# Three PSUM banks for the scan and three for the rest, the convolution in mid-unit, and u by one Silu pass, in a Mamba block with a quantised branch

## The chip, the cores and the metric

One core of one Trainium2 chip. The time is device microseconds of one launch, the median of 3 runs. Engines: TensorE (PE in the profile, PEld its weight loads), VectorE (DVE), ScalarE (ACT), GpSimd (POOL), and SyncE (SP), which here only issues DMAs. Each engine runs its own program in order; semaphores tie them together.

## The reference, cut to what matters

Eight sequences of 512 tokens and 128 channels, all in float32. Each is normalised over its channels (xn). xn then goes through a Mamba layer in both directions and through a Hadamard transform, a 4-bit rounding of each token and a ternary weight. The outputs are added to x.

```python
def _mamba_dir(xz, ...):                     # d_inner 256, state 16, dt_rank 8
    u = silu(causal_conv(x, 4 taps) + bias)
    x_dbl = einsum('bdl,kd->bkl', u, xproj_w)            # 8 rows for dt, 16 for B, 16 for C
    delta = softplus(dtproj_w @ x_dbl[:, :8] + dt_bias)
    dA = exp(einsum('bdl,dn->bdln', delta, A))
    dBx = einsum('bdl,bnl,bdl->bdln', delta, Bm, u)
    h = scan(dA, dBx)                                    # h[t] = dA[t] * h[t-1] + dBx[t]
    y = einsum('bdln,bnl->bdl', h, Cm) + Dp * u
    return y * silu(z)
xq = quantize(xn @ H)            # round(x / s), clipped to -8..7, times s; s = max|x| / 7 of a token
out = x + (out_f + out_b) @ out_proj_w.T + xq @ ternary(weight).T
```

## The kernel before, in words

**Units, slots, tiles.** The work goes in 16 units, U = 2b + d: sequence b, direction d (even units forward, odd ones backward). A unit has 8 slots s (128 channels by 4 of the 16 states), a slot has 4 tiles j of 128 partitions x 512 tokens (32 channels x 4 states), so a unit has 32 tiles. In this text k = 4s + j counts the tiles of a unit. V is the unit after U, W the one after V.

**A tile's way.** TensorE puts delta·B·u of a tile into a bank of the PSUM tensor b_ps. In slots 0 and 1 it copies delta·u there (`copies`, L864) and VectorE multiplies by B (`times_b`, L557, two tiles at once). In slots 2 to 7 it transposes four blocks (L879) of dbx_t, made in token-major form from the transposed delta·u (du_t): three state rows of four by ScalarE (`inputs_t`, L405, three instructions for each of four blocks c), the fourth by GpSimd (L688). ScalarE computes the decay exp(delta·A) (`decays`, L416) into da, a pair of buffers of 4 tiles, so it can be 8 tiles ahead. VectorE scans (L569) into hst, a ring of 4 slots. GpSimd multiplies two tiles at a time by C (`states_times_c`, L678). TensorE sums over the states into y (`sum_states`, L894).

**The next unit's preparation** runs in between. TensorE convolves (`conv`, L792, four taps for each half h of the channels) into pb, a PSUM tensor of two banks; ScalarE makes a sigmoid from a Tanh and a Copy (`u_sigmoid`, L330, L332); VectorE makes u from both (`make_u`, L539). TensorE projects it (`x_proj`, L799; `steps`, L811). The softplus goes over Abs and Relu (L351, L352), Exp (L377), a Copy (L379) and Ln (L383) on ScalarE; then VectorE has three passes over 1024 columns (`log1p`, L543 and L545; `delta`, L549). GpSimd makes delta·u (`make_du`, L694), TensorE transposes it (`du_transposed`, L819), ScalarE copies the result to du_t (`keep_dut`, L388). delta goes to HBM and comes back replicated four times (`spread` on SyncE, L234), which rep needs before V's first decay.

**Once for each sequence**, odd units have the rounding: `hadamard` (L833, TensorE), `token_max` (L514, VectorE), the scale on GpSimd (L727), `quantize` (L516, VectorE, nine instructions in a row), `project` (L848) and the residual (L580). Even units have the normalisation of the next sequence and the gate silu(z) (`z_proj`, `z_sigmoid`, `gates`), in both cases with the two banks of pb.

**What sets the order** is code written out by hand: each engine has a function `unit` with `if s == ...` lines that say after which slot half a step stands. Sequences 1 to 6 run in a hardware loop (`batches`); the first and last are written out. Everything that goes through pb waits until what was in the bank is read; in b_ps each of the 4 banks belongs to one j.

Of the kernel before, what the change touches and what calls it, by code (L numbers as in the profile page):

```python
# [35 lines left out]
def build(nc, x, win_t, wz_t, conv_w, cols, xproj_t, dt_t, a_log, wout_t, ffn_w, had, ident_d, sum_sel_d, spread_d, out):
    ctx = ExitStack()
    with ctx:
# [40 lines left out]
        xq = xn  # L79
# [37 lines left out]
        x_loaded = sem("x_loaded")  # L117
        xres_loaded = sem("xres_loaded")
# [63 lines left out]
        def batches(eng, body):
            body(0)
            with eng.Fori(1, NB - 1) as i:
                body(i)
            body(NB - 1)

        def first(b):
            return isinstance(b, int) and b == 0

        def last(b):
            return isinstance(b, int) and b == NB - 1
# [3 lines left out]
        def _(sp):  # L196
            def rows(ap, b):
                return ap[bass.ds(b, 1)].rearrange("b (c p) d -> p (b c) d", p=P)

# [846 lines left out]
```

## Time and profile before

| | us |
|---|---|
| Median of 3 runs (972.45 to 978.01) | 977.39 |
| The profiled execution, its own time | 976.08 |
| Its span | 974.0 |
| Mean granted TensorE clock, as a share of full speed | 0.864 |

The span runs from the first to the last instruction of the profiled execution; 2.1 us of its time lie outside. In the views below, "us" ahead of a row is the time since the span's start, [x <-y] is the time that the engine sat idle before the row and what ended it, "xN" the number of instructions merged. A float32 matmul of 512 columns shows as two records. Successive instructions of an engine overlap by about 0.1 us, so the distance between starts is the price in a row of them, and the duration a little more.

### The profile page before, as it was taken

The numbers are of one execution on the slowest core, as the hardware profiler recorded it, in microseconds if no ns is written. First come the engines' busy times: TensorE is split into PE (matmuls) and PEld (weight loads), VectorE is DVE, ScalarE is ACT, GpSimd is POOL, SyncE is SP. The second block draws the span as 40 slices with busy tenths as digits, with TensorE's granted clock in tenths as the row PEclk, the third lists the DMA queues.
The fourth block names the chain that finished last, engine by engine and source line by source line (L and its number), as shares of the span: only waits on it lengthen the run. The fifth ranks groups of instructions, "written<-read, shape, count | busy, mean of one in ns | idle before, by whom it ended". The sixth has DMA issues, their size and how long they took to land.

```text
span 974.0 us, 13835 instructions
## 1 busy us (share of the span) xinstructions
PE 765.9 (79%) x3873; PEld 384.4 (39%) x3873; DVE 800.2 (82%) x838; ACT 782.1 (80%) x1454; POOL 750.2 (77%) x454
## 2 busy tenths in 40 slices
PE   3486977689786977979689697878978697797994
PEld 1233443343433435334353344434443343433452
DVE  2278988898788878888888887889878887897995
ACT  2599995899878987789967998589986898878970
POOL 2159887788768977789787887878886798777994
PEclk9788988889787988979889797988978798897797
DMA  3424225070620607024070512507052070702400
GB/s 91 113 66 118 48 79 107 4 163 4 141 55 30 135 3 172 24 70 91 30 166 3 126 38 70 124 3 162 3 126 68 10 154 3 172 14 68 95 7 27
DMA packets 51433, 72.53 MB, mean 74 GB/s; under 512 B 6704, under 2 KB 19920, under 8 KB 51408
## 3 DMA queue, kind: packets, MB, share of 16 engines
q1 hardware_dynamic: 50976, 71.97, 31.6%
q10 hardware_dynamic: 432, 0.26, 0.1%
q8 instruction: 12, 0.20, 0.1%
q14 instruction: 13, 0.11, 0.0%
HBM read 60.68 MB, written 11.53 MB: 74 GB/s over the span
## 4 chain that ended last, share of the span: by engine, by line
POOL 29%; issue 27%; PE 18%; ACT 15%; DVE 8%; DMA 2%; POOLq 1%; SPq 0%; DVEq 0%; ACTq 0%
POOL hst L678 22%; PE pb L792 5%; DVE hst L569 5%; ACT da L416 4%; POOL dbx_t L688 4%; PE b_ps L879 4%; ACT dbx_t L405 2%; PE y L894 2%; PE b_ps L864 1%; PE y L891 1%; POOL t_log L694 1%; ACT xn L308 1%; PE pb L856 1%; DVE b_ps L557 1%; PE pb L811 1%
## 5 line engine op out<-in xcount | busy, mean ns | idle before, releaser
L678 POOL TENSOR_TENSOR hst<-hst,c_rep 128x1024 f32<-128x1024 f32 x256 | 600.6, 2365 | 170.8 <-DVE hst L569 170.1
L569 DVE TENSOR_TENSOR_SCAN hst<-da,b_ps 128x512 f32<-128x512 f32 x512 | 586.3, 1202 | 43.1 <-ACT da L416 21.4
L879 PE MATMUL b_ps<-ident,dbx_t 128*128 128x128 f32 x1536 | 246.6, 301 | 158.3 <-DVE hst L569 157.4
L416 ACT ACTIVATE da<-rep,neg_a 128x511 f32<-128x511 f32 x512 | 336.2, 710 | 5.8 <-DVE hst L569 3.8
L879 PEld LDWEIGHTS b_ps<-ident,dbx_t 128*128 128x128 f32 x1536 | 181.0, 151 | 281.2 <-DVE hst L569 255.7
L405 ACT ACTIVATE dbx_t<-du_t,b_t 128x256 f32<-128x256 f32 x576 | 247.0, 496 | 2.5 <-PE b_ps L879 1.7
L894 PE MATMUL y<-hst,sum_sel 128*32 128x512 f32 x1024 | 148.9, 657 | 3.0 <-POOL hst L678 3.0
L792 PE MATMUL pb<-xnt,conv_wt 128*128 128x512 f32 x256 | 121.0, 617 | 0.8 <-ACT xnt L316 0.8
L688 POOL TENSOR_TENSOR dbx_t<-du_t,b_t 128x1024 f32<-128x1024 f32 x48 | 91.3, 1903 | 2.7 <-ACT du_t L388 2.7
L864 PE MATMUL b_ps<-t_log,spread_sel 32*128 32x512 f32 x256 | 73.4, 679 | 14.3 <-POOL t_log L740 9.8
L557 DVE TENSOR_TENSOR b_ps<-b_ps,b_rep 128x1024 f32<-128x1024 f32 x64 | 78.0, 1219 | 5.4 <-PE b_ps L864 5.4
L792 PEld LDWEIGHTS pb<-xnt,conv_wt 128*128 128x128 f32 x256 | 47.2, 194 | 71.6 <-issue 71.4
L388 ACT ACTIVATE du_t<-pb 128x512 f32<-128x512 f32 x32 | 18.8, 589 | 59.7 <-PE pb L819 59.7
L891 PE MATMUL y<-u,skip 128*128 128x512 f32 x64 | 54.8, 1008 | 0.0
L539 DVE SCALAR_TENSOR_TENSOR u<-pb,col,t_exp 128x512 f32<-128x512 f32 x32 | 23.9, 746 | 36.9 <-ACT t_exp L332 36.9
L894 PEld LDWEIGHTS y<-hst,sum_sel 128*32 128x32 f32 x1024 | 21.3, 114 | 76.6 <-issue 51.6
L543 DVE SCALAR_TENSOR_TENSOR pb<-pb,t_log 128x1024 f32<-128x1024 f32 x15 | 18.5, 1233 | 39.8 <-ACT t_log L383 39.8
L864 PEld LDWEIGHTS b_ps<-t_log,spread_sel 32*128 32x128 f32 x256 | 21.7, 194 | 68.4 <-DVE hst L569 40.7
L351 ACT ACTIVATE t_exp<-pb,col 128x512 f32<-128x512 f32 x30 | 20.6, 688 | 34.2 <-PE pb L811 34.2
L330 ACT ACTIVATE t_exp<-pb,half_bias 128x512 f32<-128x512 f32 x32 | 21.9, 684 | 31.3 <-PE pb L792 31.3
L694 POOL TENSOR_TENSOR t_log<-t_pos,u 128x1024 f32<-128x1024 f32 x15 | 35.5, 2369 | 0.0
L799 PE MATMUL pb<-u,xproj 128*128 128x512 f32 x64 | 33.1, 641 | 2.3 <-DVE u L539 2.2
(111 smaller groups left out, 588.5 us busy)
## 6 DMA issues: line engine op xcount, KB each, us to landing
rep<-d_scr SPq DMA_DIRECT2D x128, 256.0 KB, 9.1
c_rep<-bc_scr SPq DMA_DIRECT2D x64, 256.0 KB, 4.8
d_scr<-t_pos SPq DMA_DIRECT2D x15, 512.0 KB, 3.0
b_rep<-bc_scr SPq DMA_DIRECT2D x64, 64.0 KB, 2.2
x_ln<-x SPq DMA_DIRECT2D x8, 256.0 KB, 3.3
x_res<-x SPq DMA_DIRECT2D x8, 256.0 KB, 2.8
out<-x_res SPq DMA_DIRECT2D x8, 256.0 KB, 7.1
conv_wt<-conv_w SPq DMA_DIRECT2D x2, 512.0 KB, 5.8
```

Source lines behind the costliest of these rows:

```text
L405: ins = nc.scalar.activation(dbx_t[(NX * d + q - 1) % 2][:, c, :, r, :], du_t[d][:, c, :, :], ACT.Copy, scale=b_t[d][:, c, n:n + 1])
L416: nc.scalar.activation(da[s % 2][:, j, 1:L], rep[d][h][:, j, 1:L], ACT.Exp, scale=neg_a[:, d, h, j, q:q + 1]).then_inc(decay_done, 1)
L557: nc.vector.tensor_tensor(b_ps[:, two, :], b_ps[:, two, :], b_rep[d][:, :].unsqueeze(1).broadcast_to([P, 2, L]), ALU.mult).then_inc(b_scal ...
L569: nc.vector.tensor_tensor_scan(hst[s % RING][:, j, :], da[s % 2][:, j, :], b_ps[:, j, :], 0.0, ALU.mult, ALU.add).then_inc(scan_done, 1)
L678: nc.gpsimd.tensor_tensor(hst[s % RING][:, two, :], hst[s % RING][:, two, :], c_rep[d][:, q:q + 1, :].broadcast_to([P, 2, L]), ALU.mult).t ...
L688: nc.gpsimd.tensor_tensor(dbx_t[(NX * d + q - 1) % 2][:, :, :, POOL_R, :], du_t[d][:, :, :, :], by_c, ALU.mult).then_inc(bm_pool, 1)
L694: nc.gpsimd.tensor_tensor(du[:, :, :], t_pos[:, :, :], u[d][:, :, :], ALU.mult).then_inc(du_ready, 1)
L792: ins = mm(pb[:, 1 - h, :], conv_wt[d][:, k, P * h:P * (h + 1)], window, start=k == 0, stop=k == TAPS - 1)
L864: mm(b_ps[:, j, :], spread_sel[at, :], du[at, h, :], start=True, stop=True).then_inc(t_filled, 1)
L879: ins = tr(b_ps[:, j, P * c:P * (c + 1)], dbx_t[(NX * d + q - 1) % 2][:, c, NJ * h + j, :, :].rearrange("p r e -> p (r e)"), ident[:, :])
L891: mm(y[:, n, :], skip[:, d, n, :], u[d][:, n, step], start=False, stop=False, skip_group_check=True)
L894: ins = mm(y[CB * j:CB * (j + 1), h, :], sum_sel[:, :], hst[s % RING][:, j, step], start=d == 0 and q == 0, stop=d == 1 and q == NQ - 1, s ...
```

## The change

- **Banks.** b_ps has 3 banks (BANKS) instead of 4, taken in turn by the running number of the tile, so TensorE may fill tile k + 3 once tile k is scanned. pb has 3 banks instead of 2. `times_b` does one tile (512 columns) at a time, one tile ahead of the scan.
- **Grain.** All engines' `unit` functions now count tiles k from 0 to 31, and place at most a few steps between two tiles. No hardware loop: the 16 units are written out.
- **Convolution.** For unit W, two units ahead, tap by tap at TensorE's k = 9, 10, 12, 13 (half 0, bank 2) and 14, 16, 17, 18 (half 1, bank 0). Before, whole halves stood at the end of U (slot 7).
- **u.** One Silu on ScalarE for each half, both at k = 23, with no VectorE pass; the Tanh, the Copy and `make_u` on VectorE are gone. The column half_bias goes too.
- **delta·u's transposes.** At TensorE's k = 20 and 22 (even U) or 20 and 21 (odd U); `keep_dut` at ScalarE's k = 25 and 27. Half n uses bank 1 + n.
- **Softplus.** Abs and Relu at k = 8 and 9, Exp at 10, the Copy at 11, Ln at 12; on VectorE the three passes at k = 9, 10 and 11 (before: in slot 3). `make_du` on GpSimd one slot half after.
- **Inputs of slots 6 and 7** (q = 3) at ScalarE's k = 17 to 20, those of V's slots 2 and 3 at 26, 27, 29 and 31.
- **Rounding.** xq now lies in x_ln. token_max, scale, inverse, round, clip and scale stand alone after VectorE's k = 24 to 29, `hadamard` at TensorE's k = 22, into bank 2. The scale is computed on VectorE.
- **Normalisation** is a sequence earlier; x of sequence 1 is loaded into x_res. Its `statistics` stand at VectorE's k = 20 of even units, its Ln and Exp (k = 12) and `normalize` (k = 22) in odd ones. `load_x` on SyncE stands behind `spread`.
- **Loads.** On SyncE the B and C loads stand ahead of the wait for delta. `x_proj` has 64 output rows instead of 128.

The core of the diff:

```diff
+G = NJ * SLOTS
+UNITS = 2 * NB
+BANKS = 3
+CONV_BANK = (2, 0)
...
-        b_ps = ps("b_ps", [P, NJ, L])
+        b_ps = ps("b_ps", [P, BANKS, L])
...
-        pb = ps("pb", [P, 2, L])
+        pb = ps("pb", [P, 3, L])
...
-            def u_sigmoid(d, V, h):
+            def make_u(V, h):
                 act.wait_ge(conv_filled, 2 * V + h + 1)
-                wait(act, delta_ready, V)
-                nc.scalar.activation(t_exp[:, h, :], pb[:, 1 - h, :], ACT.Tanh, bias=half_bias[:, d, h:h + 1], scale=0.5).then_inc(u_step, 1)
-                act.wait_ge(u_step, 2 * V + h + 1)
-                nc.scalar.activation(t_exp[:, h, :], t_exp[:, h, :], ACT.Copy, bias=0.5, scale=0.5).then_inc(u_sig, 1)
+                wait(act, sum_done, SLOTS * (V - 2) + SKIP_AT)
+                wait(act, du_ready, V - 1)
+                nc.scalar.activation(u[V % 2][:, h, :], pb[:, CONV_BANK[h], :], ACT.Silu, bias=col[:, V % 2, 0, h:h + 1]).then_inc(u_ready, 1)
...
+                    if k == 17:
+                        inputs_free(U, 3, 2 * U + 2)
+                        inputs_t(U, 3, 0)
+                    if k in (18, 19, 20):
+                        inputs_t(U, 3, k - 17, whole=k == 20)
+                    if k == 22 and d == 1 and b + 2 < NB:
+                        normalize(b + 2, x_ln)
+                    if k == 23 and conv:
+                        make_u(W, 0)
+                        make_u(W, 1)
+                    if k == 25 and nxt:
+                        keep_dut(V, 0, 2 * V + 1)
+                    if k == 26 and nxt:
+                        inputs_free(V, 1, 2 * V + 1)
+                        inputs_t(V, 1, 0)
+                    if k == 27 and nxt:
+                        keep_dut(V, 1, 2 * V + 2)
+                        inputs_t(V, 1, 1)
...
+            def inputs_free(U, q, count):
+                act.wait_ge(dut_ready, count)
+                act.wait_ge(bt_ready, U + 1)
+                wait(act, t_filled, NJ * (SLOTS * U + (4 if q == 3 else -2 if q == 1 else 0)))
...
-            def make_u(d, V, h):
-                dve.wait_ge(u_sig, 2 * V + h + 1)
-                wait(dve, sum_done, SLOTS * (V - 2) + SKIP_AT)
-                nc.vector.scalar_tensor_tensor(u[d][:, h, :], pb[:, 1 - h, :], col[:, d, 0, h:h + 1], t_exp[:, h, :], ALU.add, ALU.mult).then_inc(u_ready, 1)
...
+                    if k == 20 and d == 0 and b + 2 < NB:
+                        statistics(b + 2, x_ln)
+                    if k == 27 and d == 0:
+                        gates(b, 1)
+                    if k == 28 and d == 0:
+                        gates(b, 0)
+                    if k == 24 and d == 1:
+                        token_max(b)
...
+                wait(pe, scan_done, g - BANKS + 1)
+                mm(b_ps[:, g % BANKS, :], spread_sel[at, :], du[at, s, :], start=True, stop=True).then_inc(t_filled, 1)
...
+                    if k == 9 and nxt:
+                        log_error(V)
...
+                        if k == 21 and nxt:
+                            pe.wait_ge(u_ready, 2 * W + 1)
+                            du_transposed(V, 1)
+                        if k == 22:
+                            pe.wait_ge(dut_ready, 2 * V + 2 if nxt else 2 * U + 2)
+                            hadamard(b)
```

On ScalarE, in an odd unit before, this stands from the Ln of the next unit's softplus to the unit's end (L383 the Ln, L416 decays, L405 inputs of slots 6 and 7, L388 the copy to du_t):

```order
L383 ACT_TABLE_LOAD
L383 ACTIVATE t_log<-pb 128x1024
L416 ACT_TABLE_LOAD
L416 ACTIVATE da<-rep,neg_a 128x511 x4
L405 ACTIVATE dbx_t<-du_t,b_t 128x8x32 x3
L416 ACTIVATE da<-rep,neg_a 128x511 x2
L405 ACTIVATE dbx_t<-du_t,b_t 128x8x32 x3
...
L416 ACTIVATE da<-rep,neg_a 128x511 x8
L388 ACTIVATE du_t<-pb 128x512
```

And now, in an odd unit from the last of those inputs (L398) on; L301 is the normalisation, L323 the Silu, L409 a decay, L381 the copy to du_t:

```order
L398 ACTIVATE dbx_t<-du_t,b_t 128x8x32 x3
L409 ACTIVATE da<-rep,neg_a 128x511 x2
L301 ACTIVATE xn<-x_ln,shift,rstd 128x128 x4
L409 ACTIVATE da<-rep,neg_a 128x511
L323 ACT_TABLE_LOAD
L323 ACTIVATE u<-pb,col 128x512 x2
L409 ACT_TABLE_LOAD
L409 ACTIVATE da<-rep,neg_a 128x511 x2
L381 ACTIVATE du_t<-pb 128x512
L409 ACTIVATE da<-rep,neg_a 128x511
L398 ACTIVATE dbx_t<-du_t,b_t 128x8x32 x3
L409 ACTIVATE da<-rep,neg_a 128x511
L381 ACTIVATE du_t<-pb 128x512
```

The Silu pair has a table load on either side, and the second copy to du_t stands behind the decay of tile 27.

On TensorE, in an odd unit before, with the semaphores that each row waits for (L879 a tile's transposes, L833 the Hadamard product, L894 the sum over states):

```order
L879 MATMUL b_ps<-ident,dbx_t 128x128 [waits scan_done]
L879 MATMUL b_ps<-ident,dbx_t 128x128 x3
L833 MATMUL pb<-hadm,xnt_kept 128x128 [waits delta_ready,kept_ready]
L833 MATMUL pb<-hadm,xnt_kept 128x128 x3
L879 MATMUL b_ps<-ident,dbx_t 128x128 [waits scan_done]
L879 MATMUL b_ps<-ident,dbx_t 128x128 x3
```

And now (L875 a tile's transposes, L818 those of delta·u, L830 the Hadamard product), from k = 21 to 23:

```order
L875 MATMUL b_ps<-ident,dbx_t 128x128 [waits scan_done,bm_pool,bm_act]
L875 MATMUL b_ps<-ident,dbx_t 128x128 x3
L818 MATMUL pb<-ident,t_log 128x128 [waits du_ready,u_ready]
L818 MATMUL pb<-ident,t_log 128x128 x3
L875 MATMUL b_ps<-ident,dbx_t 128x128 [waits scan_done]
L875 MATMUL b_ps<-ident,dbx_t 128x128 x3
L830 MATMUL pb<-hadm,xnt_kept 128x128 [waits kept_ready,dut_ready]
L830 MATMUL pb<-hadm,xnt_kept 128x128 x3
L875 MATMUL b_ps<-ident,dbx_t 128x128 [waits scan_done]
L875 MATMUL b_ps<-ident,dbx_t 128x128 x3
L893 MATMUL y<-hst,sum_sel 32x512 [waits prod_done]
```

The Hadamard product waited for delta, which VectorE had made earlier; now it waits for dut_ready, the copies of the transposes that stand just ahead of it.

## Rows read from the trace of the kernel before

**Rows 1.** The page: busy time of each engine, share of the span, instructions
```profile
PE 765.9 (79%) x3873; PEld 384.4 (39%) x3873; DVE 800.2 (82%) x838; ACT 782.1 (80%) x1454; POOL 750.2 (77%) x454
```

**Rows 2.** The timeline of VectorE: first and last softplus, end of the last scan
```profile
78.18 1.23 DVE L543 SCALAR_TENSOR_TENSOR pb<-pb,t_log 128x1024 f32<-128x1024 f32 x1 [2.46 <-ACT t_log L383]
...
887.61 1.23 DVE L543 SCALAR_TENSOR_TENSOR pb<-pb,t_log 128x1024 f32<-128x1024 f32 x1 [2.52 <-ACT t_log L383]
...
961.34 0.67 DVE L575 TENSOR_TENSOR y_gated<-y,gate 128x512 f32<-128x512 f32 x1
```

**Rows 3.** The page's groups: busy, mean ns of one, idle before and its releaser
```profile
L330 ACT ACTIVATE t_exp<-pb,half_bias 128x512 f32<-128x512 f32 x32 | 21.9, 684 | 31.3 <-PE pb L792 31.3
L539 DVE SCALAR_TENSOR_TENSOR u<-pb,col,t_exp 128x512 f32<-128x512 f32 x32 | 23.9, 746 | 36.9 <-ACT t_exp L332 36.9
L543 DVE SCALAR_TENSOR_TENSOR pb<-pb,t_log 128x1024 f32<-128x1024 f32 x15 | 18.5, 1233 | 39.8 <-ACT t_log L383 39.8
```

**Rows 4.** The timeline of VectorE within sequence 4
```profile
524.33 0.67 DVE L575 TENSOR_TENSOR y_gated<-y,gate 128x512 f32<-128x512 f32 x1
...
539.84 1.23 DVE L543 SCALAR_TENSOR_TENSOR pb<-pb,t_log 128x1024 f32<-128x1024 f32 x1 [2.69 <-ACT t_log L383]
...
554.38 11.25 DVE L569 TENSOR_TENSOR_SCAN hst<-da,b_ps 128x512 f32<-128x512 f32 x10
...
615.64 0.15 DVE L518 RECIPROCAL qinv<-qscale 128x4 f32<-128x4 f32 x1
...
618.78 6.77 DVE L569 TENSOR_TENSOR_SCAN hst<-da,b_ps 128x512 f32<-128x512 f32 x6
```

**Rows 5.** The timeline of ScalarE within sequence 4
```profile
531.68 0.69 ACT L351 ACTIVATE t_exp<-pb,col 128x512 f32<-128x512 f32 x1 [2.88 <-PE pb L811]
...
536.30 1.03 ACT L379 ACTIVATE pb<-t_exp 128x1024 f32<-128x1024 f32 x1
...
539.91 1.28 ACT L416 ACT_TABLE_LOAD   x1
541.21 1.33 ACT L416 ACTIVATE da<-rep,neg_a 128x511 f32<-128x511 f32 x2
...
543.77 1.29 ACT L405 ACTIVATE dbx_t<-du_t,b_t 128x256 f32<-128x256 f32 x3
544.96 1.32 ACT L416 ACTIVATE da<-rep,neg_a 128x511 f32<-128x511 f32 x2
546.19 1.29 ACT L405 ACTIVATE dbx_t<-du_t,b_t 128x256 f32<-128x256 f32 x3
...
556.49 1.65 ACT L308 ACTIVATE xn<-x_ln,shift,rstd 128x128 f32<-128x128 f32 x4 [1.56 <-POOL shift L721]
...
561.49 0.58 ACT L388 ACTIVATE du_t<-pb 128x512 f32<-128x512 f32 x1
```

**Rows 6.** The timeline of TensorE within sequence 4
```profile
543.51 2.23 PE L879 MATMUL b_ps<-ident,dbx_t 128*128 128x128 f32 x8 [5.65 <-DVE hst L569]
545.53 3.62 PE L891 MATMUL y<-u,skip 128*128 128x512 f32 x4
...
553.88 1.06 PE L894 MATMUL y<-hst,sum_sel 128*32 128x512 f32 x8
554.88 1.53 PE L879 MATMUL b_ps<-ident,dbx_t 128*128 128x128 f32 x12
...
565.22 3.70 PE L792 MATMUL pb<-xnt,conv_wt 128*128 128x512 f32 x8
```

**Rows 7.** Busy time in two stretches (PE, PEld, DVE, ACT, POOL), granted clock, DMA share, GB/s
```profile
544.00:548.00 4.00, 4.00 (x10) 2.15 (x10) 4.00 (x5) 4.00 (x10) 2.37 (x2) 0.50 0.35 123
556.00:562.00 6.00, 4.44 (x35) 2.76 (x34) 6.00 (x6) 5.51 (x12) 5.92 (x5) 1.00 1.06 210
```

**Rows 8.** The page's DMA issues: KB each, us to landing
```profile
d_scr<-t_pos SPq DMA_DIRECT2D x15, 512.0 KB, 3.0
```

More of the change, by code:

```diff
@@ L178, in wait @@
         def wait(eng, s, count):
-            if not isinstance(count, int) or count > 0:
+            if count > 0:
                 eng.wait_ge(s, count)
[L182 to L192, printed above, removed]
         @block.sync
@@ L392, in z_sigmoid @@
+            def z_sigmoid(b, h):
                 wait(act, y_read, 2 * b)
[L393 to L402 removed]
+                act.wait_ge(z_filled, 2 * b + 2 - h)
+                nc.scalar.activation(gate[:, h, :], pb[:, h, :], ACT.Tanh, scale=0.5).then_inc(z_tanh, 1)
@@ L498, in _ @@
+            for U in range(UNITS):
+                unit(U)
             keep_xqt(NB - 1)
@@ L681, in inputs_free, with inputs_t @@
+            def inputs_t(U, q):
+                d = U % 2
                 pool.wait_ge(dut_ready, 2 * U + 2)
@@ new lines, in inputs, with skip_product @@
+                wait(pe, scan_done, g - BANKS + 1)
+                for c in range(NC):
+                    ins = tr(b_ps[:, g % BANKS, P * c:P * (c + 1)], dbx_t[(NX * d + q - 1) % 2][:, c, NJ * h + j, :, :].rearrange("p r e -> p (r e)"), ident[:, :])
+                ins.then_inc(t_filled, 1)
+            def skip_product(U, h):
+                d = U % 2
+                step = slice(None, None, -1 if d else 1)
+                pe.wait_ge(u_ready, 2 * U + 2)
+                mm(y[:, h, :], skip[:, d, h, :], u[d][:, h, step], start=False, stop=False, skip_group_check=True)
@@ L887, in sum_states @@
                     wait(pe, y_read, 2 * b - 1 + h)
-                if s == SKIP_AT - 1:
-                    pe.wait_ge(u_ready, 2 * (2 * b + d) + 2)
-                    for n in range(NH):
-                        mm(y[:, n, :], skip[:, d, n, :], u[d][:, n, step], start=False, stop=False, skip_group_check=True)
                 pe.wait_ge(prod_done, 2 * S + 2)
@@ L916, in _ @@
-            copies(0, 0, 0)
-            copies(0, 0, 1)
-            du_transposed(0, 0, delta_ready, 1)
-            du_transposed(0, 1, delta_ready, 1)
-            conv(1, 1, 0, range(TAPS), dut_ready, 1)
-            conv(1, 1, 1, range(TAPS), dut_ready, 2)
+            x_proj(0, 1)
+            steps(0, 0)
+            steps(0, 1)
+            b_transposed(0, y[:, 1, :])
+            pe.wait_ge(first_du, 1)
+            for k in range(BANKS):
+                copy(0, k)
+            pe.wait_ge(delta_ready, 1)
@@ L985, in unit @@
-                    if s == 7 and not last(b):
-                        conv(d, U + 2, 1, range(TAPS), dut_ready, 2 * V + 2)
-                    if s > 0:
-                        sum_states(b, d, s - 1)
-                    elif d == 1:
-                        sum_states(b, 0, SLOTS - 1)
-                    elif not first(b):
-                        sum_states(b - 1, 1, SLOTS - 1)
-            def body(b):
-                unit(b, 0)
-                unit(b, 1)
-            batches(pe, body)
@@ L1004, in constants @@
+            for U in range(UNITS):
+                unit(U)
+            pe.wait_ge(out_ready, NB - 1)
+            transpose_xq(NB - 1)
+            sum_states(UNITS - 1, SLOTS - 1)
+            project(NB - 1, range(NC))
 def constants():
```

757 lines of the change are left out of this document (369 added, 388 removed).

## The prediction

> **What bounds the kernel now.** The page's busy times come first [rows 1]: four engines are busy 77 to 82% of the span, so none is the bound; the loss is in hand-overs. So I ask for the loop of waits that carries one unit to the next, and measure it by one mark: the start of VectorE's first softplus pass (L543). From the first to the last there are 14 units, (887.61 - 78.18) / 14 = 57.8 us each or 115.6 for a sequence; 86.4 us follow [rows 2]. Next the groups: VectorE waits 36.9 us for the sigmoid of u and 39.8 for Ln (15 times 2.65) [rows 3]. In the timelines one reads prices by distance of starts: a scan 1.12 us (11.25 for 10, 6.77 for 6); a 512-wide VectorE pass 0.6; a 1024-wide one 1.15; the rounding's instructions from 615.64 to 618.78 are 3.14 [rows 4]. On ScalarE: three inputs 1.19 (543.77 to 544.96), two decays 1.23, so one 0.6; a table load 1.28; a 512-wide pass with bias 0.58, a plain copy 0.5; Exp or Copy over 1024 about 0.95; normalisation 1.55 [rows 5]. On TensorE at full clock: a tile's transposes 0.5, a sum 1.0, a convolution tap 0.92 [rows 6].
>
> **What goes.** VectorE loses u: 1.3 us a unit and up to 36.9 / 16 = 2.3 of waiting. The waits for b_scaled go with the tile of advance. Splitting `times_b` costs 8 x 0.6 against 4 x 1.12, +0.3. If nothing else stood in the way, that is 3 us a unit.
>
> **What comes.** ScalarE loses four passes of u (4 x 0.6) and gets two Silus at 0.58 (nearest rows: the biased passes of rows 5 and the Tanh, 684 ns [rows 3]; the trace has no Silu, bounds 0.5 and 0.7) and two table loads: 2.57 + 1.16 - 2.4 = +1.3. That is small as busy time, but it now stands in a block at k = 23, ahead of things that others wait for. So I walk the loop of an odd unit U by program order, t = 0 at the end of Ln (k = 12).
>
> 1. VectorE: three passes at 1.15 between scans 10, 11 and 12: t = 6.9.
> 2. TensorE puts tile 15 into its bank at its k = 12, behind k = 10 (tile, tap) and 11 (tile, sum, skip product: 2.4). At full clock tile 15 is there at 7.8. It will not all be at full clock: after the idle 5.65 us, 8 tile transposes took 2.23 us instead of about 1.0, with the granted clock at 0.50 of full, the 1.2 GHz level, and full speed was 1.00 [rows 6, 7]. Here TensorE idles about 3.6 to 4 us around the Ln. All at half clock gives 10.7. I take 9.0.
> 3. ScalarE may not write the inputs of slots 6 and 7 before tile 15 is transposed (same buffer), so it stops at k = 17 until 9.1. Then four inputs 4.8, decays 18 to 23 3.6, normalisation 1.55, load, two Silus, load 3.7, decays 24, 25 1.2, copy 0.5, decay 26 0.6, inputs 1.2, decay 27 0.6, second copy 0.5: 27.5.
> 4. TensorE at k = 22 waits for just that second copy (dut_ready), because the Hadamard product shares its bank. It has been idle since about 22.5. The product takes 1.0, at half clock twice that: done at 29.1.
> 5. VectorE got decay 24 at 23.6, scanned until 24.7 and stands at `token_max`: **a wait of some 4 us, in every odd unit.** Behind it are seven scans (7.85), token_max 0.6, the rounding 3.1, residual 0.6, `times_b` 0.6, and about 1.3 for tiles that TensorE, cold again, delivers late: scan 31 ends at 43.3.
> 6. V's first five scans with `times_b` 8.6, one gate pass 0.6, `steps` on TensorE 1.3: 53.8. Then ScalarE: four Abs and Relu, decays 9 to 12, B's copy (it waits 0.9), Exp, Copy, load, Ln: 10.2. **64.0.**
>
> Even unit, the same way: tile 15 at 9.0; no normalisation, so decay 24 at 22; the second gate pass on VectorE (k = 28) waits for ScalarE's k = 30, at 31.2. x for `statistics` at k = 20 is late too: SyncE issues it behind delta's store (3.0 us [rows 8]) and 2 MB of replicas, which at 210 GB/s [rows 7] take 10, and itself 1.2: at 19.8, where scan 20 is over at 17.5. It hides inside the gate's wait. Scan 31 ends at 35.8; plus 8.6, 1.3 and 9.5: **55.2.**
>
> Together 119.2 a sequence. At full clock throughout the same sum is 60.9 + 54.1 = 115.0. Before: 115.6. I take 117.6, nearer to the cold end, since rows 6 show a cold start after a gap little longer than these. The wait for Ln stays: by this sum VectorE still idles about 2.8 and 3.4 us there, as before.
>
> **Ends.** Startup: the first decay now stands behind both Silus of unit 1, whose convolution (2 x 3.7 at most [rows 6]) comes late, and behind four more table loads (5.1); the first scan comes some 8 us later, the first softplus mark, with no wait for u before it, 3.6 later: 81.8. After the last mark: 22 scans (18 before, +4.5), the last unit without waits, the same tail of 12.7 us behind the last scan (974.0 - 961.34 [rows 2]): 88.1 instead of 86.4. Span: 81.8 + 7 x 117.6 + 88.1 = 993. The profiled execution had 976.08 for a span of 974.0, and lies 1.3 under the median; so 995 us in its own terms, and I leave that as the forecast. 1.8% slower than the median of 977.39.
>
> **A rule weighed.** The load of a table took 1.28 us and the decay behind it began 0.02 later [rows 5]. The Trainium skill (ScalarE: Activation LUTs, What ACT_TABLE_LOAD costs) counts 2.66 us for each switch, a drain of about 1.38 on top. The trace disagrees; where it did hold, see the last rival.
>
> The clock: rows 6 and 7 show half speed behind a gap. The skill (TensorE: Matmul & The Clock Gate, HAM oscillation) says that a kernel whose TensorE pauses again and again pays for a cold start each time; the trace agrees.
>
> **Rivals.**
> - *The loop at full clock* (20%): the gaps are cut up finely, TensorE never gets cold, 115.0 a sequence: 81.8 + 805 + 88.1 + 2.1 = 977, no change. For it: gaps are shorter than 5.65. Against: the gap at k = 22 is 5.0 by my sum (22.5 to 27.5).
> - *The hold is hidden* (15%, faster): ScalarE runs further ahead, so the second copy comes before VectorE is through scan 24. This decides: no hold when tile 15's wait and the Silu block together cost under some 4 us less than I count. Then odd units take 57 to 58.5 and a sequence 111.2 to 113.8; with 111.5: 81.8 + 780.5 + 88.1 + 2.1 = 952. For it: VectorE's own work of a unit fell. Against: the copy is ordered behind decay 27 and the product ahead of token_max, whatever the speed.
> - *Three banks and a cold TensorE* (13%): tile, sum and skip, then tile and tap eight times, cost 1.45 us or more a step from k = 9 to 19 against a scan's 1.12; with only three tiles of advance and half clock for most of it, tiles set the pace: 119.2 plus another 2 = 121, in all 1019.
> - *Each load drains ScalarE* (2%): a further load's length, 1.28, twice in 14 units on the chain: 36 more, 1031. Against: the 0.02 us of rows 5.
>
> **How the numbers follow.** The forecast has 50%, own range 985 to 1006 (116.2 to 119.2 a sequence). A measurement of this kernel can tell about 1% from no change. Faster by over 1%: the hidden hold, 0.15. Within 1% (968 to 987): the full clock and a little of the forecast's lower side, 0.22. Slower: 0.63. The range 960 to 1014 leaves out most of the hidden hold and the upper part of the last two.
>
> **What would show it.** In the trace after: (1) the largest wait of VectorE at `token_max`, released by TensorE, 8 times 4 to 5 us; (2) TensorE before `hadamard` waiting 4 to 5 us for ScalarE's copy to du_t; (3) ScalarE before the inputs at k = 17 idle about 3 to 4 us, released by TensorE's tile; (4) waits for Ln of about 3 us, 15 times; (5) `statistics` waiting for x's DMA about 2 us; (6) marks of VectorE's first softplus pass alternating 64 and 55 us; (7) 66 table loads of 1.28 us. If (1) is absent or under 2 us, the sum is wrong and the kernel is faster; if TensorE's clock stays above 0.9, it is the first rival.

## The result, and the profile after

| | median us (lowest to highest) | ratio to the kernel before (95% interval) |
|---|---|---|
| before, same chip | 977.67 (972.45 to 978.01) | 1 |
| after | 1210.8 (1209.18 to 1213.69) | 1.2403 (1.2355 to 1.2452) |

24% slower, where 1.8% was forecast, and far outside the range. The span is 1207.6 us, the mean granted clock 0.746 (0.864 before). Each version of the kernel below ran four times; of the one with Tanh, one run in a slower state of the chip is left out. The page of the kernel after, busy time of each engine and below it the clock in 40 slices and the chain that ended last:

```profile
PE 1009.7 (84%) x3873; PEld 447.8 (37%) x3873; DVE 790.0 (65%) x877; ACT 808.0 (67%) x1454; POOL 748.6 (62%) x446
...
PEclk9759686685867858677585877858678595975878
...
PE b_ps L859 15%; ACT da L409 7%; PE y L893 7%; PE b_ps L875 7%; ACT dbx_t L398 6%; DVE hst L586 6%; PE pb L811 5%; PE pb L800 5%; PE pb L795 3%; DMA x_ln<-x 3%; PE pb L806 2%; ACT L356 2%; ACT L409 2%; PE y L882 1%; ACT t_log L356 1%
```

VectorE, ScalarE and GpSimd are busy about as before [rows 1]. TensorE is busy 244 us more, with the same 3873 instructions: they take longer. The first line of the chain is L859, the copies of delta·u into b_ps. The page's groups (busy, mean ns of one | idle before, releaser) show it from both sides, the copies and those who wait for them:

```profile
L859 PE MATMUL b_ps<-t_log,spread_sel 32*128 32x512 f32 x256 | 214.9, 1024 | 54.7 <-DVE hst L586 44.3
...
L573 DVE TENSOR_TENSOR b_ps<-b_ps,b_rep 128x512 f32<-128x512 f32 x128 | 88.7, 693 | 125.1 <-PE b_ps L859 125.1
...
L329 ACT ACTIVATE xdbl<-pb 64x512 f32<-64x512 f32 x16 | 9.4, 590 | 139.7 <-PE pb L800 139.7
...
L558 DVE SCALAR_TENSOR_TENSOR pb<-pb,t_log 128x1024 f32<-128x1024 f32 x15 | 18.5, 1232 | 94.4 <-ACT t_log L356 94.4
```

The first two in the kernel before, which ahead of the prediction had no row:

```profile
L864 PE MATMUL b_ps<-t_log,spread_sel 32*128 32x512 f32 x256 | 73.4, 679 | 14.3 <-POOL t_log L740 9.8
...
L557 DVE TENSOR_TENSOR b_ps<-b_ps,b_rep 128x1024 f32<-128x1024 f32 x64 | 78.0, 1219 | 5.4 <-PE b_ps L864 5.4
```

The copies went from 73.4 us to 214.9, VectorE's wait for them from 5.4 to 125.1 us. The wait for Ln is 94.4 / 15 = 6.3 us, against 2.65 before [rows 3]. The place is one stretch of every unit, from its start to the Ln. TensorE's timeline at the turn from an odd unit U to V (each row at its start; [x <-y] is the idle time ahead of it):

```profile
632.74 1.04 PE L875 MATMUL b_ps<-ident,dbx_t 128*128 128x128 f32 x8
...
635.72 1.12 PE L859 MATMUL b_ps<-t_log,spread_sel 32*128 32x512 f32 x2
637.32 1.09 PE L859 MATMUL b_ps<-t_log,spread_sel 32*128 32x512 f32 x2 [0.48 <-DVE hst L586]
639.63 2.04 PE L859 MATMUL b_ps<-t_log,spread_sel 32*128 32x512 f32 x2 [1.21 <-DVE hst L586]
641.60 1.94 PE L893 MATMUL y<-hst,sum_sel 128*32 128x512 f32 x8
643.46 2.07 PE L859 MATMUL b_ps<-t_log,spread_sel 32*128 32x512 f32 x2
645.46 1.97 PE L800 MATMUL pb<-u,xproj 128*64 128x512 f32 x2
...
660.18 2.07 PE L811 MATMUL pb<-xdbl,dtw 64*128 64x512 f32 x2
...
666.27 1.89 PE L806 MATMUL pb<-ident,xdbl 64*128 64x16 f32 x8
```

and the granted clock there (us, busy of PE, PEld, DVE, ACT, POOL; then the clock):

```profile
632.00:636.00 4.00, 4.00 (x34) 2.83 (x33) 4.00 (x9) 1.32 (x3) 2.52 (x2) 1.00 0.00 0
636.00:640.00 4.00, 2.31 (x5) 0.71 (x5) 4.00 (x7) 4.00 (x9) 3.76 (x3) 0.85 0.22 68
640.00:644.00 4.00, 4.00 (x11) 0.79 (x11) 3.01 (x4) 1.26 (x3) 2.31 (x2) 0.50 0.22 66
...
668.00:672.00 4.00, 4.00 (x18) 1.97 (x19) 0.00 (x0) 3.79 (x6) 2.04 (x1) 0.50 0.00 0
672.00:676.00 4.00, 2.74 (x9) 1.10 (x8) 2.10 (x2) 3.96 (x5) 0.00 (x0) 0.88 0.00 0
```

Read both together. (`x_proj` is L800, delta's products, `steps`, are L811, and the transposes of B L806.) Up to 635.7 TensorE is at full speed, and the first two copies take 1.1 us each. At 640 it is at half, the 1.2 GHz level, and for 32 us it **stays** there although it is busy without a pause; every row takes twice its time. A tile then needs one copy (2.0) and one other step (1.9), 3.9 us, where VectorE needs 1.72. The copies and projections stand ahead of the softplus in TensorE's program, so the Ln comes late by all of it, and TensorE then idles behind the Ln again. The same stretch comes in the even unit behind it (0.50 from 712 to 740).

### The profile page after: what moved, and what is told of

It reads as the page before. It is cut to its first block, busy times and chain, and to the rows that moved or that the text cites. A ratio compares the mean times of both kernels' runs of the same rounds, so it can differ in the third digit from the quotient of the medians.

```text
span 1207.6 us, 12209 instructions
## 1 busy us (share of the span) xinstructions
PE 1009.7 (84%) x3873; PEld 447.8 (37%) x3873; DVE 790.0 (65%) x877; ACT 808.0 (67%) x1454; POOL 748.6 (62%) x446
## 4 chain that ended last, share of the span: by engine, by line
PE 49%; ACT 26%; DVE 10%; issue 10%; DMA 3%; SPq 1%; POOL 1%; POOLq 0%; DVEq 0%; ACTq 0%
PE b_ps L859 15%; ACT da L409 7%; PE y L893 7%; PE b_ps L875 7%; ACT dbx_t L398 6%; DVE hst L586 6%; PE pb L811 5%; PE pb L800 5%; PE pb L795 3%; DMA x_ln<-x 3%; PE pb L806 2%; ACT L356 2%; ACT L409 2%; PE y L882 1%; ACT t_log L356 1%
## 5 line engine op out<-in xcount | busy, mean ns | idle before, releaser
L586 DVE TENSOR_TENSOR_SCAN hst<-da,b_ps 128x512 f32<-128x512 f32 x512 | 602.0, 1206 | 75.3 <-PE b_ps L875 36.7
L409 ACT ACTIVATE da<-rep,neg_a 128x511 f32<-128x511 f32 x512 | 348.2, 710 | 8.4 <-DVE hst L586 8.1
L875 PE MATMUL b_ps<-ident,dbx_t 128*128 128x128 f32 x1536 | 277.8, 313 | 74.9 <-DVE hst L586 74.9
L875 PEld LDWEIGHTS b_ps<-ident,dbx_t 128*128 128x128 f32 x1536 | 203.5, 160 | 312.9 <-DVE hst L586 160.3
L398 ACT ACTIVATE dbx_t<-du_t,b_t 128x256 f32<-128x256 f32 x576 | 248.7, 496 | 60.4 <-PE b_ps L875 60.4
L859 PE MATMUL b_ps<-t_log,spread_sel 32*128 32x512 f32 x256 | 214.9, 1024 | 54.7 <-DVE hst L586 44.3
L893 PE MATMUL y<-hst,sum_sel 128*32 128x512 f32 x1024 | 183.8, 799 | 2.9 <-POOL hst L699 2.9
L573 DVE TENSOR_TENSOR b_ps<-b_ps,b_rep 128x512 f32<-128x512 f32 x128 | 88.7, 693 | 125.1 <-PE b_ps L859 125.1
L859 PEld LDWEIGHTS b_ps<-t_log,spread_sel 32*128 32x128 f32 x256 | 53.4, 278 | 188.7 <-issue 178.4
L558 DVE SCALAR_TENSOR_TENSOR pb<-pb,t_log 128x1024 f32<-128x1024 f32 x15 | 18.5, 1232 | 94.4 <-ACT t_log L356 94.4
L811 PE MATMUL pb<-xdbl,dtw 64*128 64x512 f32 x64 | 64.1, 1105 | 0.7 <-ACT xdbl L329 0.7
L800 PE MATMUL pb<-u,xproj 128*64 128x512 f32 x64 | 61.0, 1058 | 0.8 <-ACT u L323 0.8
L830 PE MATMUL pb<-hadm,xnt_kept 128*128 128x128 f32 x64 | 15.5, 419 | 37.7 <-ACT du_t L381 37.7
L795 PEld LDWEIGHTS pb<-xnt,conv_wt 128*128 128x128 f32 x256 | 41.6, 198 | 12.0 <-issue 10.9
```

Source lines behind the costliest of these rows:

```text
L398: ins = nc.scalar.activation(dbx_t[(NX * d + q - 1) % 2][:, c, :, r, :], du_t[d][:, c, :, :], ACT.Copy, scale=b_t[d][:, c, n:n + 1])
L409: nc.scalar.activation(da[s % 2][:, j, 1:L], rep[d][h][:, j, 1:L], ACT.Exp, scale=neg_a[:, d, h, j, q:q + 1]).then_inc(decay_done, 1)
L573: nc.vector.tensor_tensor(b_ps[:, g % BANKS, :], b_ps[:, g % BANKS, :], b_rep[U % 2][:, :], ALU.mult).then_inc(b_scaled, 1)
L586: nc.vector.tensor_tensor_scan(hst[s % RING][:, j, :], da[s % 2][:, j, :], b_ps[:, g % BANKS, :], 0.0, ALU.mult, ALU.add).then_inc(scan_do ...
L795: ins = mm(pb[:, CONV_BANK[h], :], conv_wt[d][:, k, P * h:P * (h + 1)], window, start=k == 0, stop=k == TAPS - 1)
L800: ins = mm(pb[0:XC, 2, :], xproj[V % 2][:, h, :], u[V % 2][:, h, :], start=h == 0, stop=h == NH - 1)
```

## The experiments

Two questions: what does a lone copy with 32 rows cost, and does it hold the clock down? And what is left when that is gone? Times are medians; each ratio is against runs of the kernel before made beside it.

**TensorE alone.** No edit of the kernel but a program of its own. Six parts of 72 float32 matmuls of 512 columns; the first and the third 24 have the part's form (rows, columns of the weights), those between are 128 x 128. All operands are ones; with four row groups the results also go to four banks in turn, otherwise to one:

```python
r = rows * (i % (P // rows)) if groups else 0
mm(acc[0:cols, ...], w[r:r + rows, 0:cols], v[r:r + rows, :], start=True, stop=True)
```

> TensorE alone, nothing of the kernel is computed. Six parts, each after a pause of some 8 us: 24 float32 matmuls of one kind with 512 columns, 24 of 128 rows by 128 columns of weights, and again 24 of the first kind. Kinds in order: 128x128; 32 rows in one row group; 32 rows in four row groups in turn; 128 rows by 64 columns; 64 rows; 128 rows by 32 columns. Theory A (matmuls that fill few rows of the array leave the clock low): in the part with 32 rows the granted clock stays 0.50 for the whole first stretch, about 2.0 us a matmul, rises to 1.00 in the middle stretch and falls again in the third; in the 128x128 part it rises in the first stretch and stays. Theory B (only pauses of TensorE lower the clock): every kind rises to 1.00 within its first stretch and stays there, 0.9 to 1.0 us a matmul. Row groups in turn overlap: about 0.25 to 0.5 us a matmul at full clock by both.

The granted clock of its stretches (part with 32 rows in one row group from 84, 32 rows in four row groups in turn from 193, 128 rows x 64 columns from 236, 64 rows from 308; PE, PEld, ACT, POOL, clock):

```profile
84.00:100.00 16.00, 14.69 (x18) 5.85 (x19) 1.19 (x3) 0.00 (x0) 0.50 0.00 0
...
132.00:152.00 20.00, 20.00 (x47) 8.63 (x46) 0.00 (x0) 0.00 (x0) 1.00 0.00 0
...
156.00:184.00 28.00, 28.00 (x34) 10.91 (x33) 0.00 (x0) 0.00 (x0) 0.50 0.00 0
...
193.00:197.00 4.00, 3.15 (x16) 1.58 (x20) 0.76 (x2) 0.00 (x0) 0.50 0.00 0
197.00:236.00 39.00, 30.95 (x132) 13.08 (x124) 7.60 (x13) 0.00 (x0) 0.94 0.00 0
236.00:240.00 4.00, 3.80 (x5) 1.21 (x6) 0.15 (x1) 0.00 (x0) 0.51 0.01 2
240.00:300.00 60.00, 60.00 (x140) 21.29 (x138) 0.00 (x0) 0.00 (x0) 1.00 0.00 0
...
330.00:352.00 22.00, 22.00 (x27) 8.44 (x26) 0.00 (x0) 0.00 (x0) 0.50 0.00 0
352.00:372.00 20.00, 20.00 (x47) 8.45 (x46) 0.00 (x0) 0.00 (x0) 0.99 0.00 0
372.00:392.00 20.00, 20.00 (x48) 8.86 (x48) 0.00 (x0) 0.00 (x0) 1.00 0.00 0
```

Theory A came out. With 32 rows TensorE is busy all the time and stays at half; matmuls of 128 rows bring it to full; back at 32 rows it falls again, with no pause between. Few columns of weights did not do this: 128 x 64 is at full speed from 240 on, and 128 x 32 from 405 on. The same 32-row matmuls dealt to four row groups in turn are at full speed too, and run beside each other (the part took 34.1 us instead of 100.3); whether the four banks have a share in that was not run. With 64 rows it stays at half when it starts there (308 to 352), and stays at full when it comes from full (372 to 392).

Here the Trainium skill says something else. TensorE: Matmul & The Clock Gate, What's actually happening, lets the rate follow from how busy the array has been of late, so that sustained work brings it to full speed. This trace disagrees for few rows: 44 us of work without a pause, at 0.50.

**The kernel after, its copies over all rows.** The spreading matrix gets a zero-padded version for each j, so that each copy reads 128 rows and gives the same numbers.

```diff
-                at = slice(CB * j, CB * (j + 1))
-                mm(b_ps[:, g % BANKS, :], spread_sel[at, :], du[at, s, :], ...
+                mm(b_ps[:, g % BANKS, :], spread_sel[:, j, :], du[:, s, :], ...
```

> The changed kernel, with delta*u's copies into b_ps done over all 128 rows (the spreading matrix has zeros outside the tile's 32 rows) instead of 32. Same count, same columns, same waits. Theory A: TensorE's clock rises in the first half of a unit, a copy costs 0.9 instead of 2.0 us, the waits of times_b for the copies (125 us) and of ScalarE for x_proj (140 us) mostly go; 980 to 1030 us. Theory B (three banks and the chain of hand-overs keep TensorE pausing, so it is cold whatever the copies are): 1190 to 1215 us, no change.

1040.75 us, ratio 1.0662 (1.0624 to 1.0699), clock 0.906: **170 us come back from rows that hold zeros**. TensorE's timeline at the same place of the unit:

```profile
550.68 1.10 PE L858 MATMUL b_ps<-t_log,spread_sel 128*128 128x512 f32 x2 [0.91 <-DVE hst L586]
552.98 1.10 PE L858 MATMUL b_ps<-t_log,spread_sel 128*128 128x512 f32 x2 [1.21 <-DVE hst L586]
554.01 1.06 PE L892 MATMUL y<-hst,sum_sel 128*32 128x512 f32 x8
555.00 1.13 PE L858 MATMUL b_ps<-t_log,spread_sel 128*128 128x512 f32 x2
556.06 1.07 PE L800 MATMUL pb<-u,xproj 128*64 128x512 f32 x2
```

The same order with pauses as long (0.91 and 1.21 us against 0.48 and 1.21), and no fall of the clock. So the pauses alone do not bring TensorE down here; the copies of few rows do, and whether the pauses have a part in it was not run. A row costs nothing: 128 rows take 1.10, 32 rows took 1.09 to 1.12 at full speed. VectorE's wait for the copies is 14.4 us instead of 125.1. The time is 11 us above theory A's range.

**The kernel before with the same two features, one at a time.** First the pairs are taken apart: each second copy waits until the first is done.

```diff
+                    if j % 2:
+                        wait(pe, t_filled, NJ * S + j)
```

> The kernel before, with one added wait: the second copy of each pair waits for the first, so that two copies in different row groups no longer run beside each other. Theory A (a copy alone costs what a pair did, and thin matmuls one at a time leave the clock at half): 8 copies cost 0.5 us more each at full clock and more at half, and the clock falls in the first half of the units: 1010 to 1100 us, mean granted clock under 0.83. Theory B: the copies are hidden behind scans; within 1.5% of before, clock as before (0.86).

1034.8 us, ratio 1.0585 (1.0558 to 1.0612), clock 0.874. The time is as expected; the mean clock, expected under 0.83, did not fall. It did fall at one place of the unit. Where the convolution stands between lone copies it stayed at 1.00 (540 to 556 us); behind four lone copies in a row (from 553.5) it was 0.62 from 556 to 560, and `x_proj` (L799), which comes next, took 3.65 us instead of 1.98. The page's groups have it in all units, this run above, the kernel before below:

```profile
L799 PE MATMUL pb<-u,xproj 128*128 128x512 f32 x64 | 56.6, 1039 | 2.2 <-DVE u L539 2.2
```

```profile
L799 PE MATMUL pb<-u,xproj 128*128 128x512 f32 x64 | 33.1, 641 | 2.3 <-DVE u L539 2.2
```

Then the kernel before with its copies over all rows (the edit of the run above), which also ends their running side by side:

> The kernel before, with the copies over all 128 rows (zeros outside the 32), so they too no longer run beside each other, but fill the array's rows. Theory A: the copies cost 0.9 us each at full clock instead of 0.55, the clock does not fall: 970 to 1000 us, clock at least 0.86, faster than the run with copies in turn. Theory B: within 1.5% of before, as that run.

999.71 us, ratio 1.0226 (1.02 to 1.0251), clock 0.898. Losing the pairs costs the kernel before 22 us at a high clock. That is the other part of the copies' price. The run with copies in turn is 35 us slower than this one. Here `x_proj` has 613 ns in the groups, and ScalarE waits 8.5 us for it, not 33.7; these 25 us fit the cold stretch. That run is no clean price of few rows, though: its added wait also holds back the weights of the next copy, and two copies take 2.30 us there, 1.88 here.

**The kernel after, with copies asked for in twos** (tiles 1 and 2, 3 and 4, 5 and 6).

```diff
-                    if k + BANKS < G:
+                    if k in (0, 2, 4):
+                        pass
+                    elif k in (1, 3, 5):
+                        inputs(U, k + BANKS - 1)
+                        inputs(U, k + BANKS)
+                    elif k + BANKS < G:
...
```

> The changed kernel, copies still of 32 rows, but issued in twos: tiles 1 and 2 after scan 31, 3 and 4 after scan 1, 5 and 6 after scan 3, so neighbours lie in different row groups and run beside each other as in the kernel before; tile 0 stays alone. Theory A (a 32-row copy alone is what is dear and cold, in row groups in turn it is neither, as m1_rows showed with 0.47 us a matmul and a clock of 1.00): clock up, the waits of times_b for copies mostly gone, 1020 to 1100 us in spite of a tile less of advance. Rival (three banks: one bank less of advance is what made the loop slow): slower still, 1210 to 1250 us.

1146.23 us, ratio 1.174 (1.1694 to 1.1786), clock 0.800: 65 us of the 170, fewer than expected. Asked for together is not run together. TensorE's timeline at the turn from an odd to an even unit, the copies of tile 2, of 3 and 4, of 5 and of 6:

```profile
604.62 1.23 PE L859 MATMUL b_ps<-t_log,spread_sel 32*128 32x512 f32 x2 [1.21 <-DVE hst L586]
...
609.23 1.13 PE L859 MATMUL b_ps<-t_log,spread_sel 32*128 32x512 f32 x4
...
612.36 1.09 PE L859 MATMUL b_ps<-t_log,spread_sel 32*128 32x512 f32 x2 [0.41 <-DVE hst L586]
614.66 1.09 PE L859 MATMUL b_ps<-t_log,spread_sel 32*128 32x512 f32 x2 [1.22 <-DVE hst L586]
```

Tiles 3 and 4 run side by side and take 1.13 us; 2, 5 and 6 each wait for a scan of their own, and 0 and 7 have no partner. So in this unit and in the next this run makes one pair of eight copies, not three. The steps with 64 rows still stand alone too, and the next two runs ask what they add.

**Who else holds the clock down.** `steps` and `b_transposed` read 128 rows (those added are zeroed once); the copies are as in the kernel after, then in twos.

```diff
-mm(pb[:, h, :], dtw[V % 2][0:XC, P * h:P * (h + 1)], xdbl[V % 2][0:XC, :], ...
+mm(pb[:, h, :], dtw[V % 2][:, P * h:P * (h + 1)], xdbl[V % 2][:, :], ...
```

> The changed kernel; delta's products and the four transposes of B read 128 rows instead of 64 (the rows added hold zeros), the copies over the rows keep their 32 rows. Theory A (the lone 32-row copies by themselves hold TensorE at 1.2 GHz in the first half of a unit): the granted clock stays 0.50 there and the time stays within 25 us of the changed kernel, 1185 to 1215 us. Theory B (the 64-row matmuls among them matter as much, since a 64-row stretch also stood at 0.50 in the run of TensorE alone): 1060 to 1150 us and full clock after the steps. Not affected by either: 1.3 us pauses, waits for the table of Silu.

> The changed kernel with its copies asked for in twos (as in the run with pairs, which took 1146 us) and with delta's products and B's transposes over 128 rows besides. Theory A (what kept the run with pairs at 1.2 GHz were the copies that still stand alone, 0 and 7, and nothing else): no more than 20 us below 1146. Theory B (it was the 64-row products between the pairs): 1050 to 1100 us, with the granted clock at 1.00 from the steps on.

1185.19 us, ratio 1.2137 (1.2078 to 1.2195), clock 0.771; and 1118.72, ratio 1.1453 (1.1404 to 1.1502), clock 0.833. That is 26 and 28 us for the 64-row steps, in either order of the copies. The first is at the edge of theory A (the copies are enough); in the second neither theory's size came out, and its theories took for granted pairs that mostly did not form (in its timeline too only tiles 3 and 4 run side by side). In the first, TensorE's clock comes back where the steps with 128 rows stand, and only there:

```profile
644.00:650.00 6.00, 6.00 (x17) 2.31 (x10) 4.64 (x5) 2.25 (x6) 4.21 (x2) 0.50 0.68 156
650.00:656.00 6.00, 6.00 (x32) 3.37 (x32) 2.45 (x3) 5.31 (x9) 4.54 (x2) 0.81 0.01 3
656.00:662.00 6.00, 1.84 (x10) 0.97 (x9) 2.74 (x3) 5.94 (x8) 0.19 (x1) 1.00 0.00 0
```

So both kinds of few rows count; the copies come first and weigh most.

**What is left, at full rows.** The kernel after with copies over all rows stands 63 us over the kernel before. Taken from it: both copies to du_t ahead of the decay of tile 25 in odd units, and x loaded ahead of delta's store.

```diff
-                    if k == 25 and nxt:
+                    if k == (25 if d == 0 else 24) and nxt:
                         keep_dut(V, 0, 2 * V + 1)
+                        if d == 1:
+                            keep_dut(V, 1, 2 * V + 2)
```

> The full-row version (1041 us) with the two other waits of my sum taken out: in odd units both copies to du_t stand behind ScalarE's decay 24 (so the Hadamard product, and VectorE's token_max behind it, get their bank some 3 us earlier), and x of the sequence after next is loaded ahead of delta's store. My sum: 7 x 3.0 for the hold, and of 29 us of statistics' waiting up to 20 (the gate behind it waits for ScalarE too): 1000 to 1015 us. Rival: both waits only cover others that come due right behind (the Silu block on ScalarE), then 1030 to 1045.

1021.87 us, ratio 1.0461 (1.0427 to 1.0494): 19 less, between the two theories. The waits at `token_max` (33.9 us) fell to 10.1 and those of `statistics` from 28.9 to 4.5, together 48; more than half of it was paid again elsewhere. And, the other way on from the run with full rows, the Silu replaced, so that no load stands around u:

```diff
-                nc.scalar.activation(u[V % 2][:, h, :], pb[:, CONV_BANK[h], :], ACT.Silu, ...
+                nc.scalar.activation(u[V % 2][:, h, :], pb[:, CONV_BANK[h], :], ACT.Tanh, ...
```

 Theory: the loads lie on the loop of odd units (decay 24 and the copies to du_t behind them) and partly of even ones: 14 x 2.57 = 36 us of loads, of which 20 to 36 come off: 1005 to 1020. Rival: they are hidden: 1035 to 1045.

1010.86 us, ratio 1.0329 (1.0261 to 1.0397): 30 less for 32 loads fewer (34 instead of 66), which are 41 us of ScalarE, as the theory has it.

**A version that beats both.** All rows, no hold, x early, and the three softplus passes on VectorE three tiles later, where Ln is done; `make_du` and the second half of the convolution follow.

```diff
-                    if k == 9 and nxt:
+                    if k == 12 and nxt:
                         log_error(V)
...
-                    if k in (14, 16, 17, 18) and conv_next:
+                    if k in (16, 17, 18, 19) and conv_next:
```

> h1_full_nohold_x with the three softplus passes of VectorE moved from k = 9, 10, 11 to 12, 13, 14 (make_du on GpSimd half a slot later, the second half of the convolution at 16 to 19), so that VectorE scans three tiles instead of waiting 4.6 to 4.9 us for Ln. If that wait is only VectorE's (TensorE and ScalarE run on), some 3 us a unit come off: 955 to 975 us, faster than the kernel before. Rival: ScalarE and TensorE set the pace in the second half, so the wait reappears behind tile 15 or the convolution: 990 to 1015, as h1.

**953.35 us (950.95 to 956.66), ratio 0.9749 (0.9709 to 0.979)**, clock 0.952. Two of its groups:

```profile
L576 DVE TENSOR_TENSOR b_ps<-b_ps,b_rep 128x512 f32<-128x512 f32 x128 | 87.9, 687 | 16.8 <-PE b_ps L861 16.6
...
L561 DVE SCALAR_TENSOR_TENSOR pb<-pb,t_log 128x1024 f32<-128x1024 f32 x15 | 18.5, 1233 | 15.9 <-ACT t_log L356 15.9
```

68 us less than the run it starts from, and just below the 955 to 975 expected. There VectorE waited 71.9 us for Ln and ScalarE 78.3 at k = 17 for the tile; now 15.9 and 4.8. The reading that fits is one loop: three scans that need no Ln stood behind it, TensorE could not fill banks that were not scanned, and ScalarE could not write over inputs that were not transposed. (The run moves the passes, `make_du` and four taps together; their shares were not run apart.) ScalarE's idle time ahead of those inputs, in the groups, before the step and after it:

```profile
L398 ACT ACTIVATE dbx_t<-du_t,b_t 128x256 f32<-128x256 f32 x576 | 250.1, 503 | 78.3 <-PE b_ps L877 78.3
```

```profile
L398 ACT ACTIVATE dbx_t<-du_t,b_t 128x256 f32<-128x256 f32 x576 | 248.9, 498 | 4.8 <-PE b_ps L877 4.8
```

**From there, two steps back.** The copies over 32 rows again (the first edit undone); and, in another run, `BANKS = 2` for `BANKS = 3`.

> The fastest version so far (953 us) with its copies over 32 rows again, one at a time. Theory A (few rows keep the engine at 1.2 GHz, and that is what the change lost): granted clock 0.75 to 0.82, copies near 2 us each, 1090 to 1170 us. Rival (once the holds and the softplus chain are moved, the slow copies are hidden, since VectorE needs 1.72 us for each tile): 960 to 1000 us.

1129.84 us, ratio 1.1561 (1.1512 to 1.1609), clock 0.747: 176 us, about as much as the 170 in the kernel after, though the holds and softplus waits are gone. The copies' price is not hidden behind them.

> The fastest version so far (953 us) with two banks for the scans' inputs instead of three: each tile's input is asked for two scans ahead instead of three. If the third bank carries the unit over its long TensorE steps (delta's products, the convolution's taps, the projections), VectorE waits some 0.3 to 1 us at each of them, 10 to 14 a unit: 1000 to 1150 us. If two are enough at full clock, 953 to 970 us.

1149.49 us, ratio 1.1731 (1.1669 to 1.1792), clock 0.879. VectorE's timeline shows why:

```profile
611.53 0.70 DVE L576 TENSOR_TENSOR b_ps<-b_ps,b_rep 128x512 f32<-128x512 f32 x1 [1.28 <-PE b_ps L861]
612.14 1.21 DVE L589 TENSOR_TENSOR_SCAN hst<-da,b_ps 128x512 f32<-128x512 f32 x1
...
617.73 0.70 DVE L576 TENSOR_TENSOR b_ps<-b_ps,b_rep 128x512 f32<-128x512 f32 x1 [1.28 <-PE b_ps L861]
```

`times_b` runs a tile ahead of the scan. With two banks its tile can only be copied once the scan before is over, and copy, product and scan stand one behind the other: 3.1 us a tile. So the third bank is worth 196 us in this order, the fall of the clock (0.879 from 0.952) included, and at a clock of 0.952 three were enough to beat the kernel before with its four.

## Why the prediction was wrong, point by point

**The step that failed is step 6, "V's first five scans with `times_b` 8.6, ... `steps` on TensorE 1.3".** It lets VectorE set the pace from the start of a unit to `steps`. Against the trace, from Ln to Ln over the odd unit whose marks are 598.21 and 673.89 (with full rows 510.11 and 574.04):

| part | forecast | measured | with full rows |
|---|---|---|---|
| Ln to the end of scan 31 (steps 1 to 5) | 43.3 | 41.2 | 42.6 |
| to the result of `steps` (step 6, first half) | 10.5 | 23.0 | 12.1 |
| from there to the Ln (step 6, rest) | 10.2 | 11.5 | 9.2 |
| odd unit | 64.0 | 75.7 | 63.9 |
| the even unit behind it | 55.2 | 69.5 | 60.0 |

With full rows the odd unit comes out at the forecast's own number, in part by luck: 1.6 us more in the first half of step 6 meet 0.7 and 1.0 less in the other parts. Two terms were mis-sized in step 6, and they multiply. First, the copies. I took them for nothing that counts beside VectorE. In the timeline of the kernel before two copies in two row groups, four records, take 1.13 us together:

```profile
513.13 1.13 PE L864 MATMUL b_ps<-t_log,spread_sel 32*128 32x512 f32 x4
```

The change splits the pairs, and a copy alone takes 1.1 at full clock: with the other step of each tile that is 2.05 us against VectorE's 1.72. I never priced that. At full clock it is the 1.6 us of the last column; the other 10.9 went with the half clock. A rule that I passed over says it outright: TensorE: Matmul & The Clock Gate in the Trainium skill, Why this matters for your kernels, has one matmul of few rows take as long as one of 128, the gain being only that several run at once. This trace agrees (1.09 to 1.12 against 1.10). Second, the clock. I took half speed for what follows a pause and goes away with work. In the first half of a unit it did not go away for 32 us: 2.07 for a copy, 3.7 times its share of a pair.

Where the 214.6 us between my span (993) and the real one (1207.6) lie, by the row of L558 below: (1107.5 - 89.8) / 14 = 72.7 a unit instead of 58.8 makes 194.6; the start has 8.0 and the end 12.0 more. (The terms of step 3 add to 27.35, not 27.5, which moves nothing.)

```profile
L558 DVE SCALAR_TENSOR_TENSOR pb<-pb,t_log x15: 1231/1232/1233, 89.8 to 1107.5; 128x1024 f32<-128x1024 f32 x15
```

**What held.** The hold, with its place and size, and ScalarE's stop at k = 17. As a price the hold held only in part: it and the wait for x, 48 us less together, gave back 19. VectorE's waits in the kernel after (in total, times, longest):

```profile
DVE stats L516 <- DMA x_ln<-x: 37.6, 7, 5.9
...
DVE amax L523 <- PE pb L830: 33.9, 7, 4.9
```

- (1) `token_max` waits 4.85 us, where 4 to 5 were forecast; in 7 units, since the last has no unit behind it.
- (2) The Hadamard product waits 5.4 us for the copy to du_t (37.7 in all), where 4 to 5 were forecast, and step 5's scan 31 came at 41.2, against 43.3.
- (3) The inputs at k = 17 wait for the tile, 60.4 us in all, 3.8 a unit, where 3 to 4 were forecast.
- (7) The table loads are 66 of 1.28 us.
- (4) The Ln waits 6.3 us, not 3; the steps ahead of it were late.
- (5) `statistics` waits 5.4 us for x, not 2, and is not hidden by the gate's wait: a term of the even unit that was sized too small. With full rows that unit is still 4.8 over the forecast; 28.9 / 7 = 4.1 is this wait.
- (6) The marks alternate 75.7 and 69.5 us, not 64 and 55.

**The rivals.** The full clock and the hidden hold are out: clock 0.746, and the hold stands. The drain of a table load is out: loads are 1.28 and a load fewer gives back 30 / 32 = 0.9 us. The nearest was three banks with a cold TensorE (1019): tiles do set the pace at half clock. But I placed it at k = 9 to 19, where the taps stand, and at 2 us a sequence. It stands at k = 0 to 8. A sequence is 27.8 us over my sum (2 x 13.9), and 145.2 - 123.9 = 21.3 of them go with the full rows.

**What was missing from the sum.** The place of the softplus passes. I wrote that the wait for Ln "stays" and did not ask what it costs: moving the passes three tiles back, with what follows them, gave 68 us, the largest gain but the rows. It is also a piece of the change itself: the kernel before had them behind tiles 13 and 15, and the change moved them up to k = 9, 10 and 11.

## What to carry to other kernels

When a change takes matmuls of few rows out of groups that ran side by side, price each as a full one, and ask what the engine's clock does when they make up much of its work: filling the rows with zeros costs a lone matmul no time and was worth 170 to 176 us here. Where the few rows ran side by side, in the kernel before, the same filling cost 22 us. And look whether matmuls that are issued together run together: each may wait for a buffer of its own. Work that does not need a late value belongs ahead of the wait for it: here that wait also kept banks and buffers, and so two other engines. And when a sum lets one engine set the pace of a stretch, write down the other engines' time for one step of that same stretch beside it.

## What the runs showed of the hardware

- TensorE busy without a pause on matmuls of 32 rows stayed at a granted clock of 0.50 for 44 us, and fell back to 0.50 from 1.00 with no pause. With 64 rows it kept the level at which it came: 0.50 for 44 us from a cold start, 1.00 for 20 us behind 128 rows. With 128 rows and only 64 or 32 columns of weights it rose to 1.00 and stayed there.
- In the kernel before with its copies in turn, the clock stood at 0.62 right behind four lone 32-row copies in a row, with no pause; with the same copies over 128 rows it was at 1.00 there.
- The same 32-row matmuls in four row groups (and four banks) in turn rose to 1.00, and 72 matmuls took 34.1 us instead of 100.3 (24 of them, in both parts, have 128 rows).
- A float32 matmul of 512 columns takes 1.1 us at full clock, whether it reads 32 (1.09 to 1.12), 64 (1.12, `steps` in the fastest version) or 128 rows (1.10).
- A Silu of 512 columns takes 684 ns, as a Tanh of the same shape [rows 3]. It needed a table load on either side of it next to Exp, a Tanh none: 66 loads against 34.
